# A 192-column GpSimd copy behind each scatter of result rows, in a routed-expert and attention kernel

## The chip, the cores and the metric

The kernel runs on one core of one Trainium2 chip. The metric is the device time of one execution in microseconds (us). The time before is given as the median of three runs, and one more execution was taken with the hardware profiler; all rows below come from that one.

## The reference

The input is 16 sequences of 512 rows of 128 float32 numbers, so 8192 rows. A feed-forward layer, one attention layer and the same feed-forward layer again are each added to the rows. In the feed-forward layer every row is scored against 8 experts, keeps its best two, and is run through both, scaled by a gate; a shared pair of matrices runs over all rows as well.

```python
x = x + 0.5 * _L0_ffn_ref(_layernorm(x), router_DE, w_in_shared_FD, ..., w_in_eDF, w_swiglu_eDF, w_out_eFD)
x = x + _L0_attn_ref(_layernorm(x), Wq, bq, Wk, bk, Wv, bv, Wo, bo)
x = x + 0.5 * _L0_ffn_ref(_layernorm(x), ...)          # the same weights again

# inside _L0_ffn_ref, D = 128, F = 256, E = 8, TOP_K = 2
scores_aE = x_aD @ router_DE
topv_aK, topi_aK = jax.lax.top_k(scores_aE, TOP_K)
gates_Ea = sigmoid(masked_aE).T                        # only the two best are not -inf
routed_in_EaD = x_aD[None, :, :] * gates_Ea[:, :, None]
h_EaF = silu(routed_in_EaD @ w_in_eDF) * (routed_in_EaD @ w_swiglu_eDF)
out_aD = shared_out_aD + sum over E of (h_EaF @ w_out_eFD)
```

## The kernel before

The program has five parts, one behind the other: the first feed-forward front (normalise, score, route, shared matrices), the first expert stage `experts(0)`, the attention with the second front, the second expert stage `experts(1)`, and a last part that adds the expert results and the remaining shared blocks and stores the output. Each engine has its own instruction stream in program order; semaphores are the only ties.

**Routing.** In a front, GpSimd writes every row twice (once for each chosen expert) into the DRAM buffer `pairs`, with indirect DMAs of 128 rows each (`scatter`, L414 and L1021). The rows of one expert lie together, so the expert stages can read dense tiles of 256 rows. Between its scatters GpSimd also makes the second copy of the rows in SBUF (`second`, a copy of 128 columns at L405 and one of 256 columns at L1011).

**An expert stage** walks over 71 tiles of 256 rows. For tile i:
- SyncE loads it into slot `(done + i) % 10` of `XS` (L861), after the scatters of the tile that had the slot ten tiles earlier have landed (`y_sent`, L860).
- ScalarE scales the rows by their gate (`scale`, L869, two instructions), TensorE turns them (`turn`, L921), ScalarE and VectorE split the turned tile into a high and a low part (`high`, L874; L828).
- VectorE copies the expert's weights into the ring `WX`, a cast of 1024 columns from SBUF to SBUF (`weights`, L812).
- TensorE runs `up` (L913 to L915) into two banks; ScalarE applies silu to one (L888), VectorE multiplies with the other (`HT`, L822); TensorE runs `down` (L931).
- ScalarE copies the result with a factor of 0.5 into `YO`, again a ring of ten slots (`send`, L880), and counts `e_out` up.
- GpSimd waits for `e_out` and issues two indirect DMAs of 128 rows each that write `YO` to the rows of the DRAM buffer `results` (L841). Each counts `y_sent` of the slot up by 16 when it has landed. That is all that GpSimd does in these stages.

The order on VectorE in iteration i is `HT(i)`, `XSL(i+2)`, `weights(i+2)`; on ScalarE `silu(i)`, `scale(i+3)` around `high(i+2)`, `send(i-1)`; on TensorE `up(i)`, `turn(i+2)`, `down(i-1)`.

**Behind a stage.** SyncE waits until every slot's scatters have landed (L984 after the first stage, L1494 after the second), and only then loads `results` (into `Y2` at L989, into `YF` at L1500). GpSimd sums the two results of each row (L997, L1512). After the first stage attention starts from these sums. After the second, `results_added` (L1529) on VectorE stands in program order among the steps of the shared blocks.

`WT` holds the three turned attention matrices, 384 columns; it is written in the first front and only read from then on. `YO` and `XS` lie in SBUF, as does everything here that isn't called a bank.

Of the kernel before, what the change touches and what calls it, by code (L numbers as in the profile page):

```python
# [14 lines left out]
P = 128  # L15
# [24 lines left out]
def macaron(nc, batch, wq, bq, wk, bk, wv, bv, wo, bo, router, w_in_sh, w_out_sh, w_sw_sh,  # L40
# [24 lines left out]
    AB = 3  # L65
    YBUFS = 4
    EARLY = 3
    GROUPS = [(0, 1), (1, 4), (4, 8), (8, 12), (12, 16)]
    LAST_OF = {hi - 1: g for g, (lo, hi) in enumerate(GROUPS)}
    FIRST_OF = {lo: g for g, (lo, hi) in enumerate(GROUPS)}  # L70

# [6 lines left out]
    with ExitStack() as ctx:  # L78
        def sb(name, shape, dt=F32, mem=ctx):
            return mem.enter_context(nc.sbuf_tensor(name, shape, dt))  # L80

        def sem(name):
            return ctx.enter_context(nc.semaphore(name))

        def sems(name, n):
            return [sem(f"{name}{i}") for i in range(n)]
# [11 lines left out]
        WT = sb("WT", [P, 3, D])  # L98
# [11 lines left out]
        dest = sb("dest", [P, TOPK, T], I32)  # L110
        pad_rows = sb("pad_rows", [P, 2 * E, ROW])
        pad_at = sb("pad_at", [1, E], I32)
        eps_c = sb("eps_c", [P, 1])
        ints = sb("ints", [P, E * 2], I32)

# [34 lines left out]
            "q_ready k_ready v_ready weighed updated r_stats r_log r_rstd kept_split combined").split())  # L150
        x_loaded = sems("x_loaded", len(GROUPS))
        y_loaded = sems("y_loaded", 2)
        yf_loaded = sems("yf_loaded", YBUFS)
        scattered1 = sems("scattered1_", RB)
        scattered2 = sems("scattered2_", AB)
        xs_loaded = sems("xs_loaded", XB)
        y_sent = sems("y_sent", XB)
        stored = sems("stored", 2)
# [159 lines left out]
        with ExitStack() as mem:  # L318
# [13 lines left out]
            bias_lo = sb("bias_lo", [2, 2, D], mem=mem)  # L332
            spare_a = sb("spare_a", [P, len(GROUPS)], mem=mem)
            ST = sb("ST1", [P, T, 6], mem=mem)
# [5 lines left out]
            def _(sp):  # L340
                for g in range(2):
                    lo, hi = GROUPS[g]
                    sp.dma_start(X[:, BT * lo:BT * hi, :], x_t[:, BT * lo:BT * hi, :]).then_inc(x_loaded[g], 16)
# [4 lines left out]
                for n, w in enumerate((wq, wk, wv, wo)):  # L348
                    sp.dma_start(wqo[:, n, :], w).then_inc(small, 16)
                for g in range(2, len(GROUPS)):  # L350
                    lo, hi = GROUPS[g]
# [376 lines left out]
        def act_kept_high(act, b, lo, KH):  # L728
            act.wait_ge(k["xt_copied"], NB + b + 1)
            if b >= lo + 2:  # L730
                act.wait_ge(k["up1"], NB + b - 1)
            act.activation(KH[:, b % 2, :], XTR[:, W * b:W * (b + 1)], ACT.Copy).then_inc(k["xt_high"], 1)
# [10 lines left out]
        def dve_shared_step(dve, i, lo, hi, KH, KL, SSG, HID):  # L743
            if lo <= i + 2 < hi:
                b = i + 2
                dve.wait_ge(k["xt_high"], NB + b + 1)
                dve.tensor_tensor(KL[:, b % 2, :], XTR[:, W * b:W * (b + 1)], KH[:, b % 2, :].bitcast(F32),
                                  ALU.subtract).then_inc(k["kept_split"], 1)
            if lo <= i + 1 < hi:
                b = i + 1  # L750
                for c in range(FC):
                    dve.wait_ge(k[f"silu{c}"], NB + b + 1)
                    dve.tensor_tensor(HID[:, b % 2, c * W:(c + 1) * W], bank[3 + 2 * c][:, :], SSG[:, c, :], ALU.mult)\
                       .then_inc(k[f"hid{c}"], 1)
            if lo <= i < hi:
                dve.wait_ge(k["down"], NB + i + 1)
                dve.scalar_tensor_tensor(out=x_block(i), in0=bank[6][:, :].rearrange("p (j d) -> p j d", d=D),
                                         scalar=0.5, in1=x_block(i), op0=ALU.mult, op1=ALU.add)\
                   .then_inc(k["shared_added"], 1)


        def experts(ffn):
            done = NT * ffn
            with ExitStack() as own:
# [10 lines left out]
                def slot(i):  # L775
                    return (done + i) % XB
# [28 lines left out]
                @block.vector  # L805
                def _(dve):
                    dve.wait_ge(k["table_done"], ffn + 1)
                    no = Numbers(dve, "dve")

                    def weights(i):  # L810
                        e = no.expert(i)
                        dve.tensor_copy(WX[:, i % 2, :, :].rearrange("p h f -> p (h f)"),  # L812
                                        WE[:, ds(e * 4 * F, 4 * F)]).then_inc(k["e_weights"], 1)

                    no.ahead(0)
                    dve.wait_ge(xs_loaded[slot(0)], 16 * (turns(0) + 1))
                    weights(0)
                    for i in range(-2, NT):
                        if 0 <= i:
                            dve.wait_ge(k["e_silu"], done + i + 1)  # L820
                            dve.wait_ge(k["e_up1"], done + i + 1)
                            dve.tensor_tensor(HT[:, i % 2, :], bank[4 + i % 2][:, :], SG[:, i % 2, :], ALU.mult)\  # L822
                               .then_inc(k["e_hid"], 1)
                        if i + 3 < NT:
                            no.ahead(i + 3)
                        if i + 2 < NT:
                            dve.wait_ge(k["xs_high"], done + i + 3)
                            dve.tensor_tensor(XSL[:, i % 2, :], bank[i % 2][:, 0:2 * P], XSH[:, i % 2, :].bitcast(F32),  # L828
                                              ALU.subtract).then_inc(k["xs_low"], 1)
                            if i + 2:  # L830
                                weights(i + 2)
                        elif ffn and i == NT - 2:
                            dve_shared_step(dve, EARLY - 2, EARLY, NB, KH, KL, None, None)

                @block.gpsimd
                def _(pool):
                    for i in range(NT):
                        u = slot(i)
                        pool.wait_ge(k["e_out"], done + i + 1)
                        for j in range(2):  # L840
                            pool.indirect_dma_start(  # L841
                                results, bass.IndirectOffsetOnAxis(ap=XS[:, u, j, AT_DEST:AT_DEST + 1].bitcast(U32), axis=0),
                                YO[:, u, j, :], None).then_inc(y_sent[u], 16)

                @block.sync
                def _(sp):
                    rows = [sp.alloc_register(f"row{ffn}_{i}") for i in range(SLOTS)]
                    sp.wait_ge(k["table_done"], ffn + 1)
                    for r in range(NW):
                        sp.reg_load(rows, row_of[0:1, r * SLOTS:(r + 1) * SLOTS])  # L850
                        if r == 0:
                            sp.wait_ge(k["shared_added"], NB + EARLY if ffn else NB)
                            sent = scattered2 if ffn else scattered1
# [11 lines left out]
                def _(act):  # L865
# [19 lines left out]
                    for i in range(-2, NT + 1):  # L885
# [7 lines left out]
                        elif ffn and i < NT:  # L893
                            act_kept_high(act, EARLY + i + 2 - NT, EARLY, KH)
                        if i + 3 < NT:
# [5 lines left out]
                def _(pe):  # L901
# [35 lines left out]
                    for i in range(-2, NT + 1):  # L937
# [6 lines left out]
                        if 0 <= i - 1 < NT:  # L944
                            down(i - 1)

        experts(0)

        with ExitStack() as mem:
# [24 lines left out]
            GE = sb("GE", [P, 2, BT, TOPK], mem=mem)  # L974
            KH = sb("KHa", [P, EARLY, W], F32R, mem=mem)
            KL = sb("KLa", [P, EARLY, W], F32R, mem=mem)
            SSG = sb("SSGa", [P, FC, W], mem=mem)
# [215 lines left out]
            def _(act):  # L1193
# [77 lines left out]
                def gate(b):  # L1271
                    act.wait_ge(k["topped"], NB + b + 1)
                    if b >= 2:
                        act.wait_ge(k["gated"], NB + b - 1)
                    act.activation(GE[:, b % 2, :, :], TOP[:, b % 2, :, 0:TOPK], ACT.Exp, scale=-1.0)\
                       .then_inc(k["gate_raw"], 1)
# [5 lines left out]
                for i in range(-3, NB + 2):  # L1282
# [35 lines left out]
                    if 0 <= i - 2 < NB:  # L1318
                        gate(i - 2)
                for b in range(EARLY):  # L1320
                    for c in range(FC):
# [160 lines left out]
        KL = sb("KLf", [P, 2, W], F32R)  # L1482

        experts(1)

        with ExitStack() as mem:
# [75 lines left out]
```

## Time and profile before

| | |
|---|---|
| median of 3 runs | 1043.9 us (1043.36 to 1047.52) |
| the profiled execution | 1050.66 us |
| its span, from the first to the last instruction | 1048.9 us |
| busy: TensorE matmul / VectorE / ScalarE / GpSimd | 858.7 / 642.4 / 553.5 / 678.2 us |
| GpSimd in the expert stages | 284 scatters of result rows, 305.9 us |
| mean granted clock of TensorE | 0.913 of full speed |

The span is what the rows below add up to; outside of it the profiled execution has 1.8 us more. Busy time counts an engine's instructions, not its waits; a row's number in brackets is the time for which the engine stood idle just before the instruction, and what it waited for. "Issue" is idle time in which nothing that the profile shows was awaited.

### The profile page before, as it was taken

The numbers are of one execution on the slowest core, as the hardware profiler recorded it, in microseconds if no ns is written. First come the engines' busy times: TensorE is split into PE (matmuls) and PEld (weight loads), VectorE is DVE, ScalarE is ACT, GpSimd is POOL, SyncE is SP. The second block draws the span as 40 slices with busy tenths as digits, with TensorE's granted clock in tenths as the row PEclk, the third lists the DMA queues.
The fourth block names the chain that finished last, engine by engine and source line by source line (L and its number), as shares of the span: only waits on it lengthen the run. The fifth ranks groups of instructions, "written<-read, shape, count | busy, mean of one in ns | idle before, by whom it ended". The sixth has DMA issues, their size and how long they took to land.

```text
span 1048.9 us, 19476 instructions
## 1 busy us (share of the span) xinstructions
PE 858.7 (82%) x5857; PEld 741.6 (71%) x5857; DVE 642.4 (61%) x2022; ACT 553.5 (53%) x1662; POOL 678.2 (65%) x733
## 2 busy tenths in 40 slices
PE   4665775669889888929999999986798989889898
PEld 3554664559788888814777777765697988788787
DVE  6645574636455554516889998875454545545586
ACT  3212331226555655539888888862265656655432
POOL 4867776747667666763388887677266666667651
PEclk9678787779999999969999999997698989999989
DMA  9511111242233323143022211111522322332494
GB/s 231 172 39 46 44 42 37 69 89 80 82 85 92 88 82 92 59 120 98 15 77 75 63 53 37 37 39 52 103 69 83 87 83 84 86 89 69 129 259 122
DMA packets 112921, 88.01 MB, mean 84 GB/s; under 512 B 13427, under 2 KB 102133, under 8 KB 112821
## 3 DMA queue, kind: packets, MB, share of 16 engines
q1 hardware_dynamic: 94816, 51.08, 19.0%
q0 software_dynamic: 17280, 35.69, 10.3%
q8 instruction: 51, 0.84, 0.3%
q14 instruction: 50, 0.40, 0.1%
q10 hardware_dynamic: 724, 0.01, 0.0%
HBM read 43.68 MB, written 43.04 MB: 83 GB/s over the span
## 4 chain that ended last, share of the span: by engine, by line
PE 60%; DVE 10%; ACT 10%; another core or an unknown queue 9%; issue 7%; DMA 2%; POOL 2%; SPq 0%; ACTq 0%; DVEq 0%
PE bank L931 12%; PE bank L915 6%; PE bank L1395 5%; PE bank L913 5%; PE bank L914 5%; PE bank L1371 4%; PE bank L921 4%; PE bank L1381 2%; ACT XG L869 2%; PE bank L724 2%; ACT SG L888 2%; ACT PR L1246 2%; POOL results L841 2%; PE bank L206 1%
## 5 line engine op out<-in xcount | busy, mean ns | idle before, releaser
L841 POOL DMA_INDIRECT results<-YO,XS x284 | 305.9, 1077 | 166.1 <-ACT YO L880 94.0
L822 DVE TENSOR_TENSOR HT<-bank,SG 128x512 f32<-128x512 f32 x142 | 98.2, 691 | 187.1 <-PE bank L915 75.5
L913 PE MATMUL bank<-XSH,WX 128*128 128x256 f32 x568 | 175.9, 310 | 2.7 <-issue 2.7
L1021 POOL DMA_INDIRECT pairs<-PAY,POS x128 | 135.5, 1059 | 63.3 <-issue 32.9
L414 POOL DMA_INDIRECT pairs<-PAY,POS x128 | 126.2, 986 | 65.1 <-DVE POS L241 35.3
L914 PE MATMUL bank<-XSL,WX 128*128 128x256 f32 x568 | 163.3, 287 | 1.1 <-issue 1.0
L915 PE MATMUL bank<-XSH,WX 128*128 128x256 f32 x568 | 163.2, 287 | 1.0 <-issue 0.9
L931 PE MATMUL bank<-WOE,HT 128*128 x1136 | 158.5, 284 | 0.1
L931 PEld LDWEIGHTS bank<-WOE,HT 128*128 128x128 f32 x1136 | 142.2, 196 | 4.4 <-issue 1.0
L869 ACT ACTIVATE XG<-XS 128x128 f32<-128x128 f32 x284 | 113.6, 401 | 19.3 <-DMA XS<-pairs 19.3
L888 ACT ACTIVATE SG<-bank 128x512 f32<-128x512 f32 x142 | 85.1, 599 | 55.4 <-PE bank L915 44.2
L914 PEld LDWEIGHTS bank<-XSL,WX 128*128 128x128 f32 x568 | 111.9, 197 | 2.8 <-issue 2.8
L913 PEld LDWEIGHTS bank<-XSH,WX 128*128 128x128 f32 x568 | 111.8, 197 | 1.7 <-issue 1.5
L915 PEld LDWEIGHTS bank<-XSH,WX 128*128 128x128 f32 x568 | 111.0, 195 | 2.7 <-issue 2.7
L921 PE MATMUL bank<-ident,XG 128*128 128x128 f32 x284 | 59.1, 291 | 53.4 <-ACT XG L869 40.8
L812 DVE CAST WX<-WE 128x1024 fp32r x142 | 99.6, 701 | 5.3 <-DMA XS<-pairs 5.3
L880 ACT ACTIVATE YO<-bank 128x256 f32<-128x256 f32 x142 | 54.8, 386 | 88.2 <-PE bank L931 62.1
L464 ACT ACTIVATE SSG<-bank 128x512 f32<-128x512 f32 x32 | 19.1, 596 | 143.3 <-remote 75.8
L1246 ACT ACTIVATE PR<-bank,NM 128x128 f32<-128x128 f32 x256 | 90.9, 381 | 1.3 <-DVE NM L1062 1.1
L921 PEld LDWEIGHTS bank<-ident,XG 128*128 128x128 f32 x284 | 33.8, 145 | 62.3 <-ACT XG L869 47.6
L874 ACT ACTIVATE XSH<-bank 128x256 fp32r<-128x256 f32 x142 | 55.0, 387 | 41.6 <-remote 25.9
L1395 PEld LDWEIGHTS bank<-V,PT 128*128 128x128 f32 x512 | 63.5, 195 | 7.9 <-issue 7.9
(197 smaller groups left out, 1793.1 us busy)
## 6 DMA issues: line engine op xcount, KB each, us to landing
XS<-pairs SPq DMA_DIRECT2D x142, 130.0 KB
Y<-results SPq DMA_DIRECT2D x32, 256.0 KB
YF<-results SPq DMA_DIRECT2D x32, 256.0 KB, 4.1
results<-YO,XS POOLq DMA_INDIRECT x284
pairs<-PAY,POS POOLq DMA_INDIRECT x256
out<-X SPq DMA_DIRECT2D x16, 256.0 KB, 3.1
pairs<-pad_rows SPq DMA_DIRECT2D x16, 130.0 KB
pairs<-pad_rows SPq DMA_DIRECT2D x1, 1040.0 KB
```

The lines of the kernel that those rows point to most:

```text
L414: pool.indirect_dma_start(pairs, bass.IndirectOffsetOnAxis(ap=POS[:, b % RB, j, c:c + 1], axis=0), PAY[:, b % RB, c, j, :], None).then_inc ...
L841: pool.indirect_dma_start(results, bass.IndirectOffsetOnAxis(ap=XS[:, u, j, AT_DEST:AT_DEST + 1].bitcast(U32), axis=0), YO[:, u, j, :], No ...
L869: act.activation(XG[:, i % 2, j, :], XS[:, slot(i), j, 0:D], ACT.Copy, scale=XS[:, slot(i), j, AT_GATE:AT_GATE + 1]).then_inc(k["xs_scaled ...
L888: act.activation(SG[:, i % 2, :], bank[2 + i % 2][:, :], ACT.Silu).then_inc(k["e_silu"], 1)
L913: pe.matmul(ps, WX[:, i % 2, 1, w], hi, start=True, stop=False)
L914: pe.matmul(ps, WX[:, i % 2, 0, w], lo, start=False, stop=False)
L915: mm = pe.matmul(ps, WX[:, i % 2, 0, w], hi, start=False, stop=True)
L921: mm = pe.transpose(chunk(bank[i % 2], j), XG[:, i % 2, j, :], ident[:, :])
L931: mm = pe.matmul(chunk(bank[6 + i % 2], j), HT[:, i % 2, (2 * c + j) * P:(2 * c + j + 1) * P], WOE[:, ds(e * FC * D + c * D, D)], start=(c ...
L1021: pool.indirect_dma_start(pairs, bass.IndirectOffsetOnAxis(ap=POS[:, b % AB, j, c:c + 1], axis=0), PAY[:, b % AB, c, j, :], None).then_inc ...
L1246: ins = act.activation(PR[:, b % 2, a, g * P:(g + 1) * P], chunk(bank[4 + a % 2], g), ACT.Exp, bias=NM[:, b % 2, a, g:g + 1], accum_out=SU ...
L1395: mm = pe.matmul(chunk(bank[2], a), PT[:, a % 2, g * P:(g + 1) * P], V[:, b % 2, g, :], start=False, stop=(a == BT - 1 and g == G - 1))
```

## The change

Behind each of the two scatters of a tile, GpSimd copies the first 192 of the 384 columns of `WT` into a new SBUF buffer `SPARE`. Nothing reads `SPARE`. Each copy but the first waits for the copy before it, because both write the same buffer. There are 71 x 2 copies in each of the two expert stages, 284 in all.

```diff
@@ sizes and buffers
+    SPARE_W = 3 * P // 2
...
+        SPARE = sb("SPARE", [P, SPARE_W])
...
+        spare_copied = sem("spare_copied")
@@ experts(ffn), the GpSimd block
                             pool.indirect_dma_start(
                                 results, bass.IndirectOffsetOnAxis(ap=XS[:, u, j, AT_DEST:AT_DEST + 1].bitcast(U32), axis=0),
                                 YO[:, u, j, :], None).then_inc(y_sent[u], 16)
+                            copies = 2 * (done + i) + j
+                            if copies:
+                                pool.wait_ge(spare_copied, copies)
+                            pool.tensor_copy(SPARE[:, :], WT[:, :, :].rearrange("p n d -> p (n d)")[:, 0:SPARE_W])\
+                                .then_inc(spare_copied, 1)
```

## Rows read from the trace of the kernel before

**Rows 1.** The page, part 1: busy time, share of the span and instructions.

```profile
PE 858.7 (82%) x5857; PEld 741.6 (71%) x5857; DVE 642.4 (61%) x2022; ACT 553.5 (53%) x1662; POOL 678.2 (65%) x733
```

**Rows 2.** Windows, all engines: first front; then first to last scatter of each stage.

```profile
0.00:225.00 225.00, 140.73 (x781) 118.68 (x781) 130.23 (x633) 56.60 (x102) 153.90 (x225) 0.79 0.31 84
...
235.83:453.45 217.62, 187.40 (x1517) 179.40 (x1515) 111.90 (x203) 124.89 (x339) 152.89 (x142) 0.98 0.29 81
763.30:984.58 221.28, 197.16 (x1560) 189.11 (x1559) 117.14 (x210) 127.25 (x346) 152.98 (x142) 0.96 0.28 80
```

**Rows 3.** Groups by line, GpSimd alone, in the same two stage windows.

```profile
L841 POOL DMA_INDIRECT results<-YO,XS x142 | 152.9, 1077 | 78.1 <-ACT YO L880 42.1 <-issue 36.0
...
L841 POOL DMA_INDIRECT results<-YO,XS x142 | 153.0, 1077 | 88.0 <-ACT YO L880 51.9 <-issue 36.2
```

**Rows 4.** Timeline of GpSimd, 404 to 420 us: start, duration, idle before.

```profile
404.07 0.97 POOL L841 DMA_INDIRECT results<-YO,XS  x1 [1.78 <-ACT YO L880]
405.34 1.44 POOL L841 DMA_INDIRECT results<-YO,XS  x1 [0.30 <-issue]
407.09 1.31 POOL L841 DMA_INDIRECT results<-YO,XS  x1 [0.30 <-ACT YO L880]
...
411.50 0.97 POOL L841 DMA_INDIRECT results<-YO,XS  x1 [0.30 <-issue]
...
416.60 0.97 POOL L841 DMA_INDIRECT results<-YO,XS  x1 [0.30 <-issue]
419.51 0.97 POOL L841 DMA_INDIRECT results<-YO,XS  x1 [1.94 <-ACT YO L880]
```

**Rows 5.** Timeline of VectorE in the same stretch.

```profile
405.26 0.68 DVE L812 CAST WX<-WE 128x1024 fp32r x1
...
410.74 0.69 DVE L822 TENSOR_TENSOR HT<-bank,SG 128x512 f32<-128x512 f32 x1 [0.93 <-issue]
...
411.68 0.68 DVE L812 CAST WX<-WE 128x1024 fp32r x1
```

**Rows 6.** Timeline behind the first expert stage, 452 to 462 us.

```profile
452.48 0.97 POOL L841 DMA_INDIRECT results<-YO,XS  x1 [0.31 <-issue]
454.74 20.30 SPq L989 DMA_DIRECT2D Y<-results  x14
458.55 1.26 POOL L997 TENSOR_TENSOR Y<-Y 128x512 f32<-128x512 f32 x1 [5.09 <-DMA Y<-results]
...
461.25 0.87 DVE L1047 BATCH_NORM_STATS2 SA<-X 128x6 f32<-128x128 f32 x4 [16.71 <-POOL X L1002]
```

**Rows 7.** The chain that ended last, 983 to 998 us: start, duration, what.

```profile
983.62 2.22 DMA results<-YO,XS
...
987.41 5.41 DMA YF<-results
992.89 1.43 POOL YF L1512
...
997.46 0.77 PE bank L714
```

**Rows 8.** Timeline of GpSimd in the first front, 96 to 100 us.

```profile
96.93 0.97 POOL L414 DMA_INDIRECT pairs<-PAY,POS  x1 [0.30 <-issue]
97.90 0.30 POOL L405 COPY PAY<-PAY 128x128 f32<-128x128 f32 x1
98.37 0.98 POOL L414 DMA_INDIRECT pairs<-PAY,POS  x1 [0.17 <-issue]
99.65 0.97 POOL L414 DMA_INDIRECT pairs<-PAY,POS  x1 [0.30 <-issue]
```

**Rows 9.** Instructions of tile PAY: ns min/median/max, first and last start, form.

```profile
L405 POOL COPY PAY<-PAY x64: 292/303/904, 8.4 to 218.4; 128x128 f32<-128x128 f32 x64
L1011 POOL COPY PAY<-PAY x32: 387/406/473, 505.0 to 738.1; 128x256 f32<-128x256 f32 x32
```

**Rows 10.** Instructions of tiles WX and YO, same columns.

```profile
L812 DVE CAST WX<-WE x142: 680/683/936, 227.2 to 970.8; 128x1024 fp32r x142
...
L841 POOL DMA_INDIRECT results<-YO,XS x284: 953/969/1447, 235.8 to 983.6; - x142
```

**Rows 11.** Waits of SyncE's queue, 700 to 990 us: us in total, times, longest.

```profile
SPq L861 <- DMA results<-YO,XS: 50.3, 22, 5.6
```

## The prediction

> **What bounds the kernel now.** I read the page first. TensorE is the busiest engine at 82% of the span and GpSimd comes third at 65% [rows 1], which by itself says that GpSimd has time to spare. That average is over five stages, so I went on to the windows of the two expert stages, cut from the start of the first scatter to the end of the last. They last 217.62 and 221.28 us, TensorE's clock is at 0.98 and 0.96, and GpSimd is busy for 152.9 and 153.0 us with nothing but 142 scatters each [rows 2].
>
> The groups by line for GpSimd alone give the number that matters [rows 3]. A scatter takes 1.077 us in the mean. The idle time is 78.1 us in the first stage; 13.4 of it lies ahead of the first scatter (13.38 us in the timeline, outside the window), which leaves 64.7, and 152.9 + 64.7 = 217.6 closes the window. Much of this idle time is not spare: behind every scatter stands a gap of 0.30 us that nothing awaited explains [rows 4]. 141 such gaps are 42.3 us. Real slack, in which GpSimd had no result to send, is therefore 64.7 - 42.3 = **22.4 us** in the first stage, and (88.0 - 19.7) - 42.3 = **26.0 us** in the second (19.7 lies ahead of its first scatter). Per scatter that is 0.16 and 0.18 us. GpSimd is at some 90% of what it can do.
>
> The timeline shows how the slack is spread. From 404.07 to 419.51 us, 15.44 us, GpSimd issues ten scatters, five tiles; it is late behind ScalarE's results for nearly all of the stretch and catches up once, where it waits 1.94 us, of which 0.30 is the gap [rows 4]. The slack is 1.64 us in 15.44, once per five tiles, and the same in both stages with small changes.
>
> What hangs on the last scatter: behind the first stage it ends at 453.45 us, the loads of `results` start at 454.74, GpSimd sums at 458.55, VectorE starts attention at 461.25 after 16.7 us of idling [rows 6]. Behind the second the chain goes from the last scatter over its landing and the load of `YF` to GpSimd's sum and to TensorE's first matmul at 997.46 [rows 7]. So a last scatter that comes later moves all that follows one for one, in both places.
>
> **The change part by part.** *The copy itself.* Nothing is removed or moved. The trace of before has no copy of 192 columns, but has 128 columns at a median of 0.303 us and 256 columns at 0.406 [rows 9]. Between them, 192 columns take 0.355 us; I take that, with the two as the ends.
>
> *Its place behind a scatter.* In the first front GpSimd already runs this pattern: a scatter, the copy of 128 columns directly behind it with no gap, then 0.17 us, then the next scatter; without a copy the gap is 0.30 [rows 8]. Start to start the pair is 98.37 - 96.93 = 1.44 us and a bare scatter is 99.65 - 98.37 = 1.28. So the copy uses up 0.13 us of the gap. In the new place each scatter step grows by 0.355 + 0.17 - 0.30 = **0.225 us** (0.173 with the short copy, 0.276 with the long one).
>
> *The wait for the copy before.* It finished a whole scatter earlier, so the wait is over when GpSimd comes to it. Behind it stand the copy and the next scatter. I take nothing for it. If it cost 0.13 us, as much as the copy uses up of the gap, that would be 284 x 0.13 = 37 us on top; the upper end of the range allows for two thirds of it.
>
> *VectorE's weight cast.* Casts take 0.683 us in the median and up to 0.936, scatters 0.969 and up to 1.447 [rows 10]. The timelines side by side say why: the scatter at 405.34 starts 0.08 us behind a cast and takes 1.44; the one at 411.50, into which a cast falls 0.18 us after its start, takes 0.97 [rows 4, 5]. A scatter is held by a cast at some points of its run only, by (1.077 - 0.969) x 2 = 0.22 us per tile in the mean. A copy reads and writes SBUF all along, so it can be held at every point. If a copy meets a running cast it waits for the rest, half a cast or 0.34 us in the mean. There is one cast per tile and two steps of some 1.65 us, so a cast runs for 0.683/3.3 = 21% of the time, and a copy is held 0.21 x 0.34 = 0.07 us. The scatters' own stretch of 0.108 us shrinks with their share of the time, by 0.108 x (1 - 1.38/1.65) = 0.02. The difference is **0.05 us per scatter**. The ends: nothing, if they slip past each other, and a whole cast per tile in place of today's stretch, (0.68 - 0.22)/2 = 0.23, if they fall into step.
>
> The Trainium skill states this as a rule (SBUF — State Buffer, "Who interferes with whom"): a VectorE copy or cast in its two-port mode and a GpSimd instruction exclude each other for the whole instruction, and whoever issues first wins. The held scatter at 405.34 agrees; the free one at 411.50 doesn't show a block for the whole instruction. By the rule alone every meeting costs the loser the rest of the winner, and the sum would lie between my 0.05 and the 0.23.
>
> The other direction, a cast held by a copy, is at most 0.355 us, and VectorE stands idle 0.93 us ahead of its next multiplication in the steady tiles [rows 5]. It is covered there. Were that cover gone, 142 x 0.355 = 50 us would show. VectorE's other two steps of a tile read one operand from a bank.
>
> *The sum.* A scatter step grows by 0.225 + 0.05 = 0.275 us. 142 of them are 39.05 us. The slack takes up 22.4 in the first stage, because each stretch of five tiles adds 2.75 us and offers 1.64, so all of it is used after the start: **+16.7 us**. In the second stage 39.05 - 26.0 = **+13.1 us**. Together **+29.7 us** (29.8 before rounding). The start of the first scatter plus 142 steps of 1.077 + 0.30 + 0.275 = 1.652 us gives the same: 235.83 + 234.6 is 470.4, less the trailing gap and copy.
>
> On the way GpSimd falls behind by up to those amounts. SyncE already waits for landed scatters before it reloads a slot, 50.3 us in 22 waits [rows 11], so tile loads will come later and TensorE will wait for them. This doesn't add to the sum, since GpSimd then works without a pause.
>
> Against the profiled execution that is 1050.66 + 29.7 = 1080.4 us (span 1078.6). It was 6.8 us above the median of the runs. The forecast for the median is 1043.9 + 29.7, about **1074 us**.
>
> **The rivals.**
>
> *Hidden in the slack (the other side).* Place: GpSimd's idle time. A change within 0.5%, 5.2 us, needs 284 d - 48.4 to be at most 5.2, so a growth d of at most 0.19 us per scatter. For it speaks GpSimd's 65%. The short copy's 0.173 would do, without any hold. Against it, 192 columns lie above the 128 measured. It gives 1044 to 1049 us; at d = 0.173 the sum is 49.1 - 48.4 plus what the last stretch can't hide, 1045 to 1048.
>
> *Free of the cast.* d = 0.225: 142 x 0.225 = 31.95, so +9.6 and +6.0, 1059.5 us. It is the low part of my case, not another one.
>
> *In step with the cast.* Once GpSimd paces the tiles, cast and copy have the same period and their distance stops drifting. If it settles where a copy always waits for a cast, d = 0.225 + 0.23 = 0.455: 129.2 - 48.4 = +81, 1125 us; half in step (0.34) it is 1092. Against it: the scatters of before show both held and free ones in every stretch [rows 4].
>
> *TensorE becomes slow.* When tiles wait for GpSimd, TensorE is idle more. In the first front, where it was busy for 141 of 225 us, its clock stood at 0.79 against 0.98 in the stage [rows 2]. A stage's 187.4 us of matmul at 0.98 would be 232 at 0.79, still under the 234.6 of GpSimd's steps. It decides only if the clock falls below 0.78; at 0.7 it is 262 us in place of 235, +27.5 per stage, 1129 us.
>
> *VectorE held by the copies*, the 50 us above, in place of GpSimd's 30: 1094 us. The 0.93 us of idle time speaks against it.
>
> **How the numbers follow.** My case, GpSimd's steps as the pace with a growth between 0.20 and 0.35 us (1052 to 1095 us), gets 0.75, hidden in the slack 0.07, in step with the cast 0.10, TensorE's clock 0.03, VectorE held 0.04, a gain 0.01 (no term gives one). The predicted time is that of my case, 1074. The range is 1056 to 1100: growths of 0.21 to 0.37 us. It leaves out the hidden case, most of the step case and the clock. For the signs, 0.5% is about what a measurement of this kernel can tell from no change: faster 0.01, same 0.06, slower 0.93.
>
> **What would show it.** In the changed kernel's profile there should be 284 copies at 0.36 to 0.45 us, some up to 1.0; the idle time before a scatter should be 0.17 almost everywhere; waits of L841 for `YO` should fall from 24 per stage to fewer than five. The stage windows should be about 234 us each. L841 should hold a much larger share of the chain, waits of SyncE L861 for landed scatters should be longer, and TensorE's busy time unchanged. The first load of `Y2` should come near 471 us. The prediction is wrong if idle GpSimd time beyond the gap remains (then the pace is another engine's), if copies take above 0.5 us in the mean, or if the gap behind a copy isn't 0.17.

## The result, and the profile after

The changed kernel takes **1069.9 us** in the median, against 1043.6 us for the kernel before: a ratio of **1.025, 95% interval 1.020 to 1.030**. It is slower, by 26.3 us, where 1074 us (+30) was forecast. The profiled execution took 1066.8 us with a span of 1065.0.

The page of the changed kernel, parts 1 and 4, against [rows 1]:

```profile
PE 862.4 (81%) x5857; PEld 736.3 (69%) x5857; DVE 658.0 (62%) x2022; ACT 549.0 (52%) x1662; POOL 794.9 (75%) x1017
...
POOL 39%; PE 30%; DVE 9%; issue 7%; another core or an unknown queue 7%; ACT 6%; DMA 2%; SPq 0%; ACTq 0%; DVEq 0%
POOL results L844 26%; POOL SPARE L850 12%; PE bank L1403 5%; PE bank L1379 4%; PE bank L1389 2%; PE bank L727 2%; ACT PR L1254 2%; PE bank L209 2%; PE bank L201 1%; PE bank L657 1%; PE bank L1356 1%; PE bank L1368 1%; PE bank L1345 1%; DVE PAY L1117 1%
```

GpSimd is busy 117 us longer: the copies take 130.1 us, and the scatters of result rows 14.1 us less than before (291.8 in place of 305.9). TensorE's busy time is the same within 4 us. The chain that ended last now lies on GpSimd for 39% of the span. Its two main lines are the scatter (L844, L841 before) and the new copy (L850). The windows from the first to the last scatter, against [rows 2]:

```profile
226.25:460.19 233.94, 191.16 (x1517) 178.56 (x1515) 118.73 (x203) 121.90 (x339) 210.00 (x283) 0.96 0.27 76
...
766.28:1001.16 234.88, 206.11 (x1613) 192.63 (x1611) 127.38 (x215) 128.79 (x352) 210.93 (x283) 0.99 0.27 75
```

The stages grew by 233.94 - 217.62 = 16.3 and 234.88 - 221.28 = 13.6 us, 29.9 together (16.7 + 13.1 = 29.8 was forecast). The spans of the two profiled executions differ by 16.1 us only, since the parts outside the stages were 13.8 us shorter in this one: the first front alone took 226.3 us up to the first scatter where it had taken 235.8. The changed kernel has no new instruction there. So the windows are the sharper measure, and they are what I compare below.

Inside the first stage's window the chain that ended last shows the change of pace most plainly. Before, 74% of it lay on TensorE's lines and 1.6% on the scatters; after, 94% lies on GpSimd's scatters, its copies and the gaps between them. In the second stage GpSimd and its gaps are practically the whole chain.

```profile
by line: PE bank L931 29.7%; PE bank L915 14.4%; PE bank L914 10.6%; PE bank L913 10.6%; issue 9.1%; PE bank L921 8.3%; ACT XG L869 4.7%; ACT SG L888 4.5%; another core or an unknown queue 3.2%; POOL results L841 1.6%; ACT XSH L874 1.5%; AC
```

```profile
by line: POOL results L844 58.6%; POOL SPARE L850 25.8%; issue 9.7%; PE bank L939 2.2%; DMA results<-YO,XS 1.0%; PE bank L923 1.0%; PE bank L922 0.9%; PE bank L921 0.9%; PE bank L929 0.5%; ACT YO L888 0.2%
```

GpSimd's groups by line in the first stage, and the waits there, against [rows 3]:

```profile
L844 POOL DMA_INDIRECT results<-YO,XS x142 | 146.3, 1030 | 37.9 <-issue 23.3 <-ACT YO L888 14.6
L850 POOL COPY SPARE<-WT 128x192 f32<-128x192 f32 x141 | 63.9, 453 | 0.5
```

```profile
ACT XG L877 <- DMA XS<-pairs: 82.3, 52, 3.2
DVE XSL L831 <- ACT XSH L882: 66.8, 42, 3.2
...
POOL results L844 <- issue: 23.3, 140, 0.2
POOL results L844 <- ACT YO L888: 14.6, 2, 14.4
```

The gap in front of a scatter is 23.3/140 = 0.17 us. GpSimd waits for a result of ScalarE only before the first scatter (14.4 us) and for the length of one gap later on; before, it did so 24 times. All slack is gone. In its place ScalarE waits 82.3 us in 52 waits for tile loads, and SyncE waits longer for landed scatters before it reloads a slot:

```profile
SPq L869 <- DMA results<-YO,XS: 159.3, 54, 4.2
```

That is for both stages; before it was 92.2 us in 39 waits. It is the ring of ten slots passing GpSimd's pace back to the others. The timeline in the middle of the stage shows the steps, and a copy that a cast holds:

```profile
275.27 0.98 POOL L844 DMA_INDIRECT results<-YO,XS  x1 [0.17 <-issue]
276.26 0.35 POOL L850 COPY SPARE<-WT 128x192 f32<-128x192 f32 x1
276.77 0.98 POOL L844 DMA_INDIRECT results<-YO,XS  x1 [0.17 <-issue]
...
277.76 0.90 POOL L850 COPY SPARE<-WT 128x192 f32<-128x192 f32 x1
277.78 0.68 DVE L815 CAST WX<-WE 128x1024 fp32r x1
```

The copy at 276.26 takes 0.35 us; the one at 277.76, which starts together with a cast, takes 0.90, and the scatter behind it starts that much later. Where the cast starts a little further behind the copy, the cast is the one that is held:

```profile
374.57 0.36 POOL L850 COPY SPARE<-WT 128x192 f32<-128x192 f32 x1
...
374.61 0.88 DVE L815 CAST WX<-WE 128x1024 fp32r x1
```

Of the 142 copies 39 take more than 0.42 us in the first stage and 43 in the second. All of these but one end 0.18 to 0.21 us behind the end of a cast. The instructions of the new tile, and the cast's, against [rows 9, 10]:

```profile
L850 POOL COPY SPARE<-WT x284: 350/355/895, 227.2 to 1001.2; 128x192 f32<-128x192 f32 x142
```

```profile
L815 DVE CAST WX<-WE x142: 681/692/1161, 216.5 to 976.1; 128x1024 fp32r x142
```

Behind both stages what follows still starts as far behind the last scatter as in [rows 6, 7], within 0.3 us:

```profile
459.21 0.98 POOL L844 DMA_INDIRECT results<-YO,XS  x1 [0.17 <-issue]
460.20 0.35 POOL L850 COPY SPARE<-WT 128x192 f32<-128x192 f32 x1
461.49 7.28 SPq L997 DMA_DIRECT2D Y<-results  x6
465.24 1.26 POOL L1005 TENSOR_TENSOR Y<-Y 128x512 f32<-128x512 f32 x1 [4.68 <-DMA Y<-results]
...
467.94 0.87 DVE L1055 BATCH_NORM_STATS2 SA<-X 128x6 f32<-128x128 f32 x4 [26.80 <-POOL X L1010]
```

```profile
1000.18 2.25 DMA results<-YO,XS
...
1009.16 1.27 POOL YF L1520
```

From the end of the last scatter to the first load it is 1.30 us, against 1.29 before.

### The profile page after: what moved, and what is told of

It is laid out like the page before. It is cut to its first block, busy times and chain, and to the rows that moved or that the text cites. A ratio compares the mean times of both kernels' runs of the same rounds, so it can differ in the third digit from the quotient of the medians.

```text
span 1065.0 us, 19760 instructions
## 1 busy us (share of the span) xinstructions
PE 862.4 (81%) x5857; PEld 736.3 (69%) x5857; DVE 658.0 (62%) x2022; ACT 549.0 (52%) x1662; POOL 794.9 (75%) x1017
## 4 chain that ended last, share of the span: by engine, by line
POOL 39%; PE 30%; DVE 9%; issue 7%; another core or an unknown queue 7%; ACT 6%; DMA 2%; SPq 0%; ACTq 0%; DVEq 0%
POOL results L844 26%; POOL SPARE L850 12%; PE bank L1403 5%; PE bank L1379 4%; PE bank L1389 2%; PE bank L727 2%; ACT PR L1254 2%; PE bank L209 2%; PE bank L201 1%; PE bank L657 1%; PE bank L1356 1%; PE bank L1368 1%; PE bank L1345 1%; DVE PAY L1117 1%
## 5 line engine op out<-in xcount | busy, mean ns | idle before, releaser
L844 POOL DMA_INDIRECT results<-YO,XS x284 | 291.8, 1027 | 76.9 <-issue 46.6
L831 DVE TENSOR_TENSOR XSL<-bank,XSH 128x256 fp32r<-128x256 f32 x142 | 60.0, 423 | 161.1 <-ACT XSH L882 142.1
L939 PEld LDWEIGHTS bank<-WOE,HT 128*128 128x128 f32 x1136 | 138.7, 192 | 8.7 <-issue 1.7
L850 POOL COPY SPARE<-WT 128x192 f32<-128x192 f32 x284 | 130.1, 458 | 1.0
L815 DVE CAST WX<-WE 128x1024 fp32r x142 | 107.9, 760 | 5.0 <-DMA XS<-pairs 5.0
L467 ACT ACTIVATE SSG<-bank 128x512 f32<-128x512 f32 x32 | 19.1, 595 | 124.5 <-remote 62.7
```

The lines of the kernel that those rows point to most:

```text
L844: pool.indirect_dma_start(results, bass.IndirectOffsetOnAxis(ap=XS[:, u, j, AT_DEST:AT_DEST + 1].bitcast(U32), axis=0), YO[:, u, j, :], No ...
L850: pool.tensor_copy(SPARE[:, :], WT[:, :, :].rearrange("p n d -> p (n d)")[:, 0:SPARE_W])\
L939: mm = pe.matmul(chunk(bank[6 + i % 2], j), HT[:, i % 2, (2 * c + j) * P:(2 * c + j + 1) * P], WOE[:, ds(e * FC * D + c * D, D)], start=(c ...
```

## The experiments

The kernel before isn't equally fast in all sets of runs: its median was 1043.6 us in the first comparison and 1043.8 in the last, but 1069.1 us in the set with one copy, 320 columns and the two kernels with the cast cut (set A), and 1068.4 in that with two buffers, both behind the second, 64 columns and ScalarE (set B). The cause is open; set A ran on the same chip as the last set. So totals are compared as ratios within a set, and windows are given for each stage.

There is no profile of the kernel before from sets A and B, so its windows there can only be estimated. In the four profiles of set A all that lies outside the two windows comes to 608 to 612 us of the span, and in the profile of the kernel before it was 610.0. If it was as much for the kernel before in set A, the two windows share what is left of its span of 1067.3 us: 228 to 230 us each, in place of 218 and 221. For set B (608 to 619 us outside) the same sum gives 224 to 229. By this estimate most of the 25 us lie in the stages of the kernel before. They don't appear in stages that GpSimd paces: the two-buffer kernel of set B has the changed kernel's windows.

| experiment | ratio to before (95%) | windows, us |
|---|---|---|
| one copy per tile | 0.998 (0.994 to 1.002) | 223.9, 225.6 |
| 320 columns | 1.041 (1.035 to 1.048) | 248.3, 247.7 |
| before, cast cut | 1.009 (1.007 to 1.011) | 231.7, 231.0 |
| after, cast cut | 0.998 (0.995 to 1.001) | 226.4, 225.7 |
| two buffers | 1.015 (1.006 to 1.023) | 233.9, 235.0 |
| both copies behind the second scatter | 1.009 (1.006 to 1.012) | 229.8, 231.8 |
| 64 columns | 0.999 (0.995 to 1.003) | 223.7, 225.6 |
| copies on ScalarE | 1.018 (1.011 to 1.026) | 234.5, 233.5 |
| before, again | 1.001 (0.997 to 1.005) | 218.1, 217.5 |
| after, again | 1.030 (1.026 to 1.035) | 234.2, 235.2 |
| before, fewer matmuls | 0.994 (0.990 to 0.998) | 216.9, 216.5 |
| after, fewer matmuls | 1.034 (1.026 to 1.041) | 235.1, 235.6 |

**Before and after once more.** The two kernels unchanged, in one set, 1044.7 and 1075.2 us.

> The kernel before, unchanged, as a yardstick: in the last eight runs it took 1068 to 1069 us in the median, 25 us more than in the first comparison. Its windows say where: if the fronts and the attention alone are longer, they stay at 218 and 221 us and the slack is what the forecast took; if TensorE's stretches inside the stages are longer too, they are at 223 to 230 us and there is more slack for the copies.

> The changed kernel, unchanged, beside the one before on one chip. GpSimd's steps as the pace: windows of 234 and 235 us again, whatever the windows of before are here, since a step of scatter, copy and gap takes 1.65 us anyway. If the windows of before are longer here (223 to 230), the difference in the total shrinks to 10 to 24 us, 1.009 to 1.022; if they are 218 and 221, it stays at 1.025. Rival, a cost that comes on top of whatever paces the stage: 1.025 in either case and windows of 16 us over those of before.

```profile
236.52:454.59 218.07, 187.92 (x1517) 179.07 (x1515) 111.52 (x203) 124.74 (x339) 153.74 (x142) 0.98 0.29 81
...
761.97:979.50 217.53, 194.71 (x1560) 183.57 (x1559) 116.00 (x210) 128.46 (x346) 152.87 (x142) 1.00 0.29 81
```

```profile
231.33:465.51 234.18, 191.62 (x1517) 182.64 (x1515) 119.07 (x203) 123.77 (x339) 210.25 (x284) 0.94 0.28 76
...
773.43:1008.63 235.20, 206.19 (x1613) 195.33 (x1611) 128.80 (x215) 130.00 (x352) 211.24 (x284) 0.98 0.27 75
```

The windows grew by 16.1 and 17.7 us, 33.8 together, the median by 30.5. The stage times of the changed kernel repeat within 0.4 us; those of before within 0.5 and 3.8. What the change costs depends on the slack that an execution of the kernel before happens to have.

**Two copies against one, and the width.**

```diff
-                            copies = 2 * (done + i) + j
...
+                            if j == 1:
+                                if done + i:
+                                    pool.wait_ge(spare_copied, done + i)
```

> One copy of 192 columns per tile in place of two, behind the second scatter only. GpSimd's steps as the pace: a tile then costs GpSimd 0.28 us more, 19.5 us per stage, less than the slack of 22.4 and 26.0 us, so the copies hide: first-to-last-scatter windows of 218 to 221 and 221 to 224 us, 1044 to 1049 us in all, no more than 0.5% above before. Rival, a cost for each copy wherever it stands (VectorE held, or contention in general): half of the 26 us that 284 copies cost, 1057 us, windows of 226 and 228 us.

```diff
-    SPARE_W = 3 * P // 2
+    SPARE_W = P // 2
```

> 64 columns in place of 192 in all 284 copies. A copy takes some 0.25 us, a step grows by 0.25 - 0.13 + 0.04 = 0.16 us, 23 us per stage against a slack of 22.4 and 26.0: windows of 218 to 222 and 221 to 224 us, 1044 to 1050 us. Rival, a fixed cost per copy that the width hardly changes: windows of 230 us, 1063 us.

```diff
-    SPARE_W = 3 * P // 2
+    SPARE_W = 5 * P // 2
```

> 320 columns in place of 192 in all 284 copies. GpSimd's steps as the pace: a copy takes 0.46 us unheld, a step grows by 0.46 - 0.13 + 0.05 = 0.38 us, all of which shows since the slack is used up: windows of (1.38 + 0.38) x 142 = 249 us, so +30 us against the changed kernel, about 1100 us. Rival, a cost in proportion to the columns: 26 x 320/192 = 44 us over before, 1087 us, windows of 239 us. Rival, TensorE's clock falls once it waits: windows well above 250 us.

In their sets one copy per tile and two narrow ones cost nothing that can be measured; 320 columns cost 4.1%, 42 us in a set where before had 1069 (the windows are the 249 us expected, the total of 1110.7 is 11 us above). The groups by line in the first stage, for one copy, for 64 and for 320 columns:

```profile
L844 POOL DMA_INDIRECT results<-YO,XS x142 | 151.0, 1063 | 63.8 <-ACT YO L888 32.9 <-issue 30.9
L850 POOL COPY SPARE<-WT 128x192 f32<-128x192 f32 x70 | 26.2, 374 | 0.2
```

```profile
L844 POOL DMA_INDIRECT results<-YO,XS x142 | 153.2, 1079 | 52.5 <-ACT YO L888 31.8 <-issue 20.7
L850 POOL COPY SPARE<-WT 128x64 f32<-128x64 f32 x141 | 37.4, 266 | 0.5
```

```profile
L844 POOL DMA_INDIRECT results<-YO,XS x142 | 144.6, 1018 | 40.3 <-issue 23.4 <-ACT YO L888 16.9
L850 POOL COPY SPARE<-WT 128x320 f32<-128x320 f32 x141 | 79.9, 567 | 0.4
```

With the first two, waits for ScalarE's result remain (32.9 and 31.8 us, of which 17.2 and 19.8 lie before the first scatter); with 320 columns none remains beyond the first, and the step is 1.018 + 0.567 + 0.17 = 1.755 us, times 142 = 249 us, the window of 248.3. This fits a threshold and not a price per copy: half of the copies cost nothing, and two thirds more columns cost 13 to 14 us more per stage than the changed kernel has. The test is weaker than it looks, since the kernel before had more slack in these sets if the estimate above holds. What the kernels' own rows add to it: with one copy GpSimd's work and unexplained gaps in the first window are 177.1 + 30.9 = 208 us, with 64 columns 190.5 us of work and 141 gaps of 0.17 us, 214.5 us. Both would fit into 217.6 too. The windows of 223.7 to 225.6 us lie 1.6 to 2.9 us above the upper ends that were forecast, and not above the estimate for the kernel before in these sets.

**The wait for the copy before, and the place of the copies.**

```diff
-                            if copies:
-                                pool.wait_ge(spare_copied, copies)
+                            if copies > 1:
+                                pool.wait_ge(spare_copied, copies - 1)
```

The copy of j = 1 goes to another buffer, which is idle in the stage.

> The two copies of a tile write to two buffers in turn, so each waits for the copy two back and not for the one before. If the wait costs nothing, as forecast: like the changed kernel, windows of 234 us, within 0.5% of 1070 us. Rival, the wait for the preceding copy costs something like 0.13 us: up to 37 us faster, windows of 216 to 225 us.

The windows, 233.9 and 235.0, are those of the changed kernel to 0.2 us. The wait costs nothing. The ratio is only 1.015 since the kernel before took 1068.4 us in that set. The median of 1085.3 misses "within 0.5% of 1070": outside the windows this execution was 23 us longer than the changed kernel's (619.3 against 596.2), and the edit touches nothing there.

```diff
+                            if j == 1:
+                                if done + i:
+                                    pool.wait_ge(spare_copied, 2 * (done + i))
+                                for h in range(2):
+                                    pool.tensor_copy(spares[h], ...).then_inc(spare_copied, 1)
```

> Both copies of a tile stand behind its second scatter, in two buffers; none between the scatters. GpSimd's steps as the pace, with the gap of 0.30 us shortened only where a copy follows: the first scatter keeps its gap of 0.30, the second has 0.17 behind two copies, so a tile costs 0.13 us more than in the changed kernel, 9 us per stage: windows of 243 us, 1088 us. Rival, only the sum of copy work counts: like the changed kernel, windows of 234 us.

```profile
340.75 1.09 POOL L846 DMA_INDIRECT results<-YO,XS  x1 [0.30 <-issue]
341.84 0.36 POOL L853 COPY SPARE<-WT 128x192 f32<-128x192 f32 x1
342.13 0.35 POOL L853 COPY XTR<-WT 128x192 f32<-128x192 f32 x1
342.65 0.98 POOL L846 DMA_INDIRECT results<-YO,XS  x1 [0.17 <-issue]
```

```profile
L846 POOL DMA_INDIRECT results<-YO,XS x142 | 146.9, 1035 | 47.8 <-issue 33.4 <-ACT YO L891 14.4
L853 POOL COPY SPARE<-WT 128x192 f32<-128x192 f32 x70 | 29.1, 416 | 0.2
L853 POOL COPY XTR<-WT 128x192 f32<-128x192 f32 x70 | 24.5, 350 | 0.0
```

The gaps are as expected, 0.30 behind a bare scatter and 0.17 behind copies, yet the windows shrank by 4.1 and 3.1 us instead of growing by 9. Two terms were wrong. The second copy starts 0.29 us behind the first though that takes 0.36, and in the mean the pair costs 0.06 less than its sum; and the copies were held less, 0.416 and 0.350 us in the mean against 0.453. The sum of this kernel's own rows, 2 x 1.035 + 0.30 + 0.17 + 0.416 + 0.350 - 0.06 = 3.25 us per tile, is 230.5 us for 71, and the window is 229.8.

**The cast.** From the third tile of a stage on, VectorE casts 8 of 1024 columns, so the later tiles' expert weights are left out.

```diff
+                        n = 4 * F if i < 2 else 8
-                        dve.tensor_copy(WX[...].rearrange("p h f -> p (h f)"),
-                                        WE[:, ds(e * 4 * F, 4 * F)])...
+                        dve.tensor_copy(WX[...].rearrange("p h f -> p (h f)")[:, 0:n],
+                                        WE[:, ds(e * 4 * F, n)])...
```

> The kernel before with VectorE's weight cast cut to 8 of 1024 columns from the third tile of each stage on (the experts' weights of later tiles are left out, so it computes something else). Scatters should all take 0.97 us, since only the cast stretched them; GpSimd's slack grows by 15 us per stage. If TensorE paces the stages before, the windows stay at 215 to 220 us and the time at 1036 to 1044 us. If GpSimd or VectorE paced them already, the windows fall to 205 us or less.

> The changed kernel with the same cut of the cast (later tiles' expert weights left out). A step of GpSimd is then 0.97 + 0.355 + 0.17 = 1.50 us, 212 us per stage, just under what the stages take before: windows of 215 to 222 us, all copies at 0.355 us, at most 8 us above the kernel before without the cast. Rival, copies cost the same whatever VectorE does (their wait, the in-order queue): 26 us above the kernel before without the cast, windows of 232 us.

```profile
L842 POOL DMA_INDIRECT results<-YO,XS x142 | 137.3, 967 | 116.8 <-ACT YO L881 82.7 <-issue 34.0
```

```profile
L845 POOL DMA_INDIRECT results<-YO,XS x142 | 139.4, 982 | 58.4 <-ACT YO L889 39.2 <-issue 19.2
L851 POOL COPY SPARE<-WT 128x192 f32<-128x192 f32 x141 | 49.9, 354 | 0.4
```

Without the cast the scatters take 0.967 us and the copies 0.354 in the mean: the cast is all that stretches either. With the cast cut the copies no longer cost time; the kernel with them was even faster, by 10 us. GpSimd's step is then 0.982 + 0.354 + 0.17 = 1.51 us, 214 us for 142, and another loop sets the window of 226.4 us, 4 us above the upper end that was forecast. The kernel before was expected at 215 to 220 us without its casts, or below, and has windows of 231.7 and 231.0: it got slower by 0.9% against the kernel before of that set, whose windows are estimated above at 228 to 230. Giving GpSimd and VectorE less to do didn't speed the stage up. I have no cause for it, nor for the 10 us between the two kernels.

**Fewer matmuls.** The matmuls of L914 (the low part of the rows) are left out, which lowers the accuracy.

```diff
-                                pe.matmul(ps, WX[:, i % 2, 0, w], lo, start=False, stop=False)
```

> The kernel before without the matmuls that multiply the high weights with the low part of the rows (a third of the work of L913 to L915 is left out, the result loses accuracy). TensorE paces the stages of before, so the windows fall: to 196 to 205 us, where GpSimd's 142 steps of 1.38 us become the next pace. If GpSimd paced them already, the windows stay within 3 us of those of before.

> The changed kernel with the same matmuls left out. GpSimd paces its stages, so TensorE's lighter work gives nothing: windows of 232 to 236 us, and 30 to 38 us per stage over the same cut of the kernel before (142 steps that are 0.23 to 0.28 us longer, with no slack left to hide them). Rival, TensorE or VectorE still paces the changed kernel: windows fall below 225 us.

```profile
233.84:450.77 216.93, 167.45 (x1241) 159.93 (x1239) 112.79 (x204) 123.43 (x339) 152.99 (x142) 0.90 0.29 81
...
758.06:974.54 216.48, 170.20 (x1275) 160.27 (x1274) 115.31 (x210) 125.03 (x346) 152.59 (x142) 0.94 0.29 82
```

```profile
235.19:470.29 235.10, 165.81 (x1241) 150.45 (x1239) 118.14 (x204) 120.12 (x339) 211.06 (x283) 0.94 0.27 75
```

The changed kernel doesn't care for 25 us less of matmul in the first stage: 235.1 us, GpSimd's pace. The kernel before doesn't either: its windows fell by 1.1 us each against "before, again", where 13 to 22 were expected if TensorE had been the pace. So my account of the kernel before in these two expectations, TensorE as its pace, is wrong. GpSimd isn't it alone, as it still waits 44.3 us for ScalarE's results (17.2 of them before the first scatter). Its chain still lies on TensorE's lines for the most part, so neither the chain nor one engine's busy time names the pace here. What sets the 218 us stays open. For that reason the second half of the last expectation missed: the changed kernel was to be 30 to 38 us per stage above the same cut of the kernel before, and it is 18.2 and 19.1.

**The copies on ScalarE.**

```diff
                         act.activation(YO[...], bank[6 + i % 2][:, 0:2 * D], ACT.Copy, scale=0.5)...
+                        for h in range(2):
+                            copies = 2 * (done + i) + h
+                            if copies:
+                                act.wait_ge(spare_copied, copies)
+                            act.activation(SPARE[:, :], WT[...][:, 0:SPARE_W], ACT.Copy)...
```

> ScalarE makes the two copies of a tile behind its result copy, GpSimd makes none. GpSimd as the pace: it is as free as before and the scatters take 1.08 us; what is left is 0.9 us per tile more on ScalarE, which is idle for 93 of 218 us: windows of 218 to 228 us, 1044 to 1060 us. Rival, that reading and writing SBUF beside the stage costs whatever engine does it: windows of 234 us, 1070 us.

```profile
236.03:470.57 234.54, 194.56 (x1517) 184.98 (x1515) 114.13 (x203) 161.28 (x480) 144.98 (x142) 0.95 0.27 75
```

```profile
DVE HT L825 <- ACT SG L897: 63.1, 48, 4.5
POOL results L844 <- ACT YO L883: 54.8, 28, 3.2
```

The windows are 234.5 and 233.5, the rival's number, and 218 to 228 was missed. The rival's reason isn't shown by that: GpSimd's scatters take 1.02 us here and GpSimd waits 28 times for ScalarE, so it has slack and another loop is the pace. The two copies (0.76 us together in the timeline) stand between a tile's result copy and the silu of the next, VectorE waits 63.1 us in 48 waits for the silu (25.7 in 19 before), and the copies lie on the chain of the first window for 7.5% of it, 17.6 us. ScalarE is 69% busy, so its mean doesn't show this either. That the window equals GpSimd's pace looks like chance, but that was not tested: this run by itself doesn't refute the rival. In the changed kernel the chain does, since it is filled by GpSimd's own steps.

## Why the prediction was right

**What bounds the kernel.** Reading GpSimd as some 90% used in spite of its 65% on the page was right, and is what the whole forecast rests on. It didn't need to know what paces the kernel before, and that is still not known. The slack, 22.4 and 26.0 us, was used up as reckoned: 24 waits for ScalarE fell to the one before the first scatter.

**The step.** Forecast 1.652 us for scatter, copy and gap. Measured in the first stage 1.030 + 0.453 + 0.17 = 1.653, in the second 1.025 + 0.465 + 0.17 = 1.66. That the first agrees to 0.001 us is luck in part: two terms were too small by 0.03 us each and cancelled.

- *The copy unheld.* 0.355 us between the rows for 128 and 256 columns; 0.355 in the median.
- *The gap.* 0.17 in place of 0.30, taken from the first front; 23.3/140 = 0.17.
- *The wait for the copy before.* Nothing; the run with two buffers shows it.
- *The cast.* The net was right and its parts were both too small. A copy is held 0.453 - 0.355 = 0.10 us in the mean (forecast 0.07), because 27% and 30% of the copies are held where the forecast had 21%. A scatter takes 0.05 less than before (forecast 0.02). The sum is +0.05 as forecast. That it is the cast is shown by the run without it, in which both holds are gone. The Trainium skill's rule (SBUF — State Buffer, "Who interferes with whom"), by which whoever issues first keeps the other out, fits the copies and casts: held copies end 0.2 us behind a cast, and a cast that starts 0.04 us behind a copy takes 0.88 us while the copy takes 0.36. The order can't be read to the last hundredths: the copy at 277.76 is recorded 0.02 us ahead of the cast and is the one that waits. Casts grew from 99.6 to 107.9 us in all, but little of that is the copies' doing: of the 44 casts above 0.75 us in the two stages, 33 began 0.3 to 0.7 us behind the start of a scatter, among them the longest of 1.161 us, and 11 met a copy.

**The sum.** +16.7 and +13.1 us forecast, +16.3 and +13.6 measured between the two profiled executions, +16.1 and +17.7 in the second pair. The medians moved by 26.3 and 30.5 us. The 4 us between 1074 and 1069.9 are less than the changed kernel's own spread, 1061.8 to 1073.1 without its slowest run. That the stages' sum came within 0.1 us of the forecast in the first pair is chance as well: in the second pair it is 4 us off.

**One for one behind the stages.** Right in both places; from the last scatter to VectorE's first instruction of attention it is 7.8 us in both kernels. The first load of `Y2` came at 461.49 and not near 471, since this execution's first front was 9.6 us shorter.

**The rivals.** Hidden in the slack: refuted here, but this is what seems to happen with one copy per tile or 64 columns, as the bound of 0.19 us of growth per scatter says (one copy per tile is (0.374 - 0.13)/2 = 0.12 per scatter, 64 columns 0.266 - 0.13 = 0.14). In step with the cast: no; one copy of every tile would be held for a whole cast then, 71 in a stage, and it is 39 and 43, for 0.36 us in the mean. TensorE slow: its clock in the stages was 0.96 and 0.99, and 25 us less of matmul changed nothing. VectorE held: its casts grew by 8 us in all, and the window is met by GpSimd's steps alone.

## What to carry to other kernels

An engine at 65% on the page can be nearly full in one stage: take its busy time and its unexplained gaps from the windows of that stage, and count as slack only what is left. Work added to an engine in program order is free up to this slack and costs its full price from there on, so add up whole steps (operation, gap, and what holds it) and compare them with the stage's own time. When a front or a set of runs wanders by more than the effect, compare the windows of the stage that the change touches, not the totals.

## What the runs showed of the hardware

- A GpSimd copy of 192 columns that meets a VectorE cast of 1024 columns takes up to 0.895 us in place of 0.355; 81 of the 82 held copies ended 0.18 to 0.21 us behind the end of a cast. With the cast cut down to 8 columns, copies take 0.354 us in the mean and scatters 0.98.
- A GpSimd copy right behind a scatter shortens the gap to the next scatter from 0.30 to 0.17 us, and makes that next scatter take 0.98 instead of 0.97 us. Of two copies in a row the second starts 0.29 us behind a first one of 0.36.
- A copy of 64 columns takes 0.244 us in the median, 192 take 0.355 and 320 take 0.463: 0.19 us and 0.85 ns per column.
- With VectorE's casts nearly all cut the kernel before was 0.9% slower, though that freed 0.11 us per scatter on GpSimd. Unexplained.
